# Offsets of both axes in one load, the fourth convolution behind the first batch, and all column spreads on VectorE

## The reference, cut to what matters

```python
off = conv2d(x, ow, ob).reshape(Bn, K, 2, Hh, Ww)          # K = 9 taps, y and x offsets
cy = iy[None, None, :, None] + dy[None, :, None, None] + off[:, :, 0]
cx = ix[None, None, None, :] + dx[None, :, None, None] + off[:, :, 1]
# bilinear samples of x at (cy, cx), zero outside the image
samp = gather(y0i, x0i, (1 - wy) * (1 - wx)) + gather(y0i, x0i + 1, (1 - wy) * wx) \
     + gather(y0i + 1, x0i, wy * (1 - wx)) + gather(y0i + 1, x0i + 1, wy * wx)
out = jnp.einsum('bckhw,ock->bohw', samp, w.reshape(w.shape[0], Cin, K))
```

## Time and profile before

| | us |
|---|---|
| median of 3 executions | 921.49 (920.93 to 923.78) |
| profiled execution, its own time | 921.92 |
| its span | 919.9 |
| TensorE busy | 649.7 (71%) |
| VectorE busy | 579.8 (63%) |
| ScalarE busy | 467.0 (51%) |
| GpSimd busy | 376.6 (41%) |

### The profile page before, as it was taken

How to read it: one execution, slowest core, us unless ns; L and a number is a source line. 1 busy time by engine, 2 the same in 40 slices (tenths; PEclk the granted TensorE clock), 3 DMA queues, 4 the chain that set the end, 5 groups by cost and what they waited for, 6 DMA issues and landing times.

```text
span 919.9 us, 30354 instructions
## 1 busy us (share of the span) xinstructions
PE 649.7 (71%) x13944; PEld 451.3 (49%) x13944; DVE 579.8 (63%) x755; ACT 467.0 (51%) x623; POOL 376.6 (41%) x383
## 2 busy tenths in 40 slices
PE   2409999999987484758887379757875767909483
PEld 1104555567853373546666246436654555706252
DVE  6894162221344995758988434896886777677365
ACT  3505433432423765757778131675776777632513
POOL 6000000000038347897886003859778888300000
PEclk9858999999999897888888779988887878958787
DMA  4000000000079637664664007966556665000002
GB/s 152 0 0 2 2 4 3 2 16 4 16 182 280 238 115 247 218 209 155 222 210 148 1 2 193 343 197 215 193 164 233 217 217 201 26 0 4 1 3 92
DMA packets 37994, 108.76 MB, mean 118 GB/s; under 512 B 16244, under 2 KB 20980, under 8 KB 29672
## 3 DMA queue, kind: packets, MB, share of 16 engines
q0 software_dynamic: 23616, 86.82, 28.2%
q1 hardware_dynamic: 14248, 19.97, 7.0%
HBM read 91.84 MB, written 19.65 MB: 121 GB/s over the span
## 4 chain that ended last, share of the span: by engine, by line
PE 37%; DVE 24%; POOL 12%; DMA 11%; issue 8%; ACT 7%; SPq 0%; DVEq 0%; ACTq 0%; POOLq 0%
PE psum L1222 12%; DMA arena<-offsets_by_batch 10%; PE psum L1269 7%; POOL arena L1500 6%; POOL arena L417 6%; PE psum L1198 5%; PE psum L1303 4%; PE psum L1415 3%; DVE arena L729 3%; DVE arena L730 3%; DVE arena L728 2%; PE psum L1281 2%; PE psum L1422 2%; ACT arena L1068 1%; PE psum L1235 1%
## 5 line engine op out<-in xcount | busy, mean ns | idle before, releaser
L1303 PE MATMUL psum<-arena 64*64 64x297 f32 (+4 forms) x4512 | 237.4, 369 | 122.6 <-ACT arena L1078 94.4
L1303 PEld LDWEIGHTS psum<-arena 64*64 64x64 f32 x4512 | 185.3, 149 | 174.6 <-issue 112.9
L417 POOL TENSOR_SCALAR arena<-arena 128x384 f32<-128x384 f32 (+2 forms) x68 | 180.7, 2681 | 47.3 <-PE psum L1303 47.2
L1500 POOL DMA_DIRECT2D arena<-offsets_by_batch x256 | 151.2, 633 | 42.4 <-DVE arena L730 33.1
L1471 POOL DMA_DIRECT2D columns<-arena x16 | 10.1, 757 | 298.3 <-DVE arena L694 243.3
L1222 PE MATMUL psum<-arena 32*32 32x512 f32 x3456 | 115.0, 597 | 0.3 <-DVE arena L652 0.3
L728 DVE SCALAR_TENSOR_TENSOR arena<-arena 128x792 f32<-128x792 f32 (+3 forms) x96 | 94.0, 979 | 25.3 <-ACT arena L1068 24.8
L1055 ACT ACTIVATE arena<-arena 128x2304 f32<-128x2304 f32 (+1 forms) x32 | 71.5, 2235 | 60.5 <-DMA arena<-offsets_by_batch 60.5
L1269 PE MATMUL psum<-arena 32*32 32x512 f32 x2304 | 86.3, 641 | 21.8 <-issue 16.0
L1067 ACT ACTIVATE arena<-arena 128x792 f32<-128x792 f32 (+3 forms) x96 | 84.5, 880 | 33.4 <-DMA arena<-offsets_by_batch 33.4
L1078 ACT ACTIVATE arena<-psum 128x792 f32<-128x792 f32 (+1 forms) x96 | 82.7, 861 | 32.4 <-PE psum L1303 25.2
(11 more groups left out here) (138 smaller groups left out, 688.9 us busy)
## 6 DMA issues: line engine op xcount, KB each, us to landing
arena<-offsets_by_batch POOLq DMA_DIRECT2D x224, 288.0 KB, 5.2
arena<-offsets_by_batch POOLq DMA_DIRECT2D x32, 312.0 KB, 5.7
offsets<-arena SPq DMA_DIRECT2D x32, 256.0 KB, 7.8
offsets_by_batch<-offsets SPq DMA_DIRECT2D x92, 48.0 KB, 2.8
columns<-arena POOLq DMA_DIRECT2D x8, 320.0 KB, 6.7
arena<-columns POOLq DMA_DIRECT2D x8, 320.0 KB, 7.5
arena<-in_x SPq DMA_DIRECT2D x4, 512.0 KB, 5.3
out<-arena SPq DMA_DIRECT2D x8, 256.0 KB, 2.2
```

The lines of the kernel that those rows point to most:

```text
L417: return eng.tensor_scalar(ap(z_at(a, 0) + i * C, [[64, NBK], [ZROW, b - a], [1, C]]), ap(ZC + c % 2 * ZCS + (a - CHUNKS[c][0]) * C, [[ZCB ...
L1303: ins = t_.matmul(ps_t(s, bank + r, first * K * w, many * K * w), window, ap(g_at(unit, d0) + first * TW + s * w, [[GS + TW, many], [SLOTS ...
L1500: g.dma_start(cols(in_at(n, axis), in_rows(n) * W, 64 * r + 32 * half, 32), bass.AP(batch_d.tensor, (axis * B + 4 * r) * NB * INS + n * IN ...
```

## The change

Three things are edited.

1. *One load for both axes.* In DRAM the arranged offsets of a batch now hold x and y side by side, and so does the buffer on chip (`in_at`). `load_batch` issues four transfers of 576 KB instead of eight of 288 KB, on one semaphore (`s_in`), and ScalarE's distances wait for all of it. `arrange_batch` issues one copy per axis: six for a batch in the middle instead of three.
2. *The fourth convolution.* TensorE runs `convolve(3)` between the units of batch 0 and those of batch 1. ScalarE copies it out behind unit 2 and the y terms of unit 6. VectorE takes its reach and bounds behind batch 1 instead of behind batch 0. It has bank 4 like the third one, and its bounded offsets go to a place of their own (`bounded_at`), so that they no longer wait for the store of quarter 1. SyncE arranges batch 4 ahead of the store of quarter 3. ScalarE waits for the store and the reach of quarter 3 at unit 24 instead of unit 6.
3. *The spreads.* All four images are spread by VectorE, `for i in range(4)`. GpSimd has no arithmetic left in the loop; it issues `load_batch(n)` and, behind the loads of batches 4 and 8, `load_windows`.

```diff
@@ -207,11 +207,16 @@
         NATS = 4 * CH
         assert 8 * CH <= SPAR and 2 * NATS <= min(N, SPAR)
 
+        def bounded_at(m):
+
+
+            return RAW + NATS if m == 3 else D1 + m % 2 * NATS
+
         PROJ = T_PAD[3] + PADN - 2 * CH
 
         xt_d = nc.dram_tensor("columns", [2, XQ, 4, H, C], F32, kind="Internal").ap()
         off_d = nc.dram_tensor("offsets", [2, B * KP, H, W], F32, kind="Internal").ap()
-        batch_d = nc.dram_tensor("offsets_by_batch", [2, B, NB, INS], F32, kind="Internal").ap()
+        batch_d = nc.dram_tensor("offsets_by_batch", [B, NB, 2 * INS], F32, kind="Internal").ap()
         flag_d = nc.dram_tensor("reach", [P, 8], F32, kind="Internal").ap()
 
         psum = ctx.enter_context(nc.psum_tensor("psum", [P, 8, CH], F32))
...
@@ -298,7 +302,7 @@
 
         def conv_bank(m):
 
-            return 4 if m % 2 == 0 else 0
+            return 0 if m == 1 else 4
 
         HALF = N // 2
         HALF_ROWS = H // 2 + 2
...
@@ -463,9 +467,11 @@
 
                 def taps(ky, at, step, row, rows):
 
-                    sp.dma_start(bass.AP(batch_d.tensor, n * INS + at, [[NB * INS, 2 * B], [step, 3], [1, rows * W]]),
-                                 bass.AP(off_d.tensor, 3 * (ky + 1) * N + row * W,
-                                         [[KP * N, 2 * B], [N, 3], [1, rows * W]])).then_inc(s_ar[n % 2], 16)
+                    for axis in range(2):
+                        sp.dma_start(bass.AP(batch_d.tensor, (2 * n * ER + axis * in_rows(n)) * W + at,
+                                             [[2 * NB * INS, B], [step, 3], [1, rows * W]]),
+                                     bass.AP(off_d.tensor, (axis * B * KP + 3 * (ky + 1)) * N + row * W,
+                                             [[KP * N, B], [N, 3], [1, rows * W]])).then_inc(s_ar[n % 2], 16)
 
                 for ky in (-1, 0, 1):
                     row = SLOTS * n - ky
...
@@ -493,8 +499,8 @@
                 arrange_batch(L, 2)
                 store_offsets(L, 2)
                 arrange_batch(L, 3)
+                arrange_batch(L, 4)
                 store_offsets(L, 3)
-                arrange_batch(L, 4)
                 sp.wait_ge(s_am, L + 1)
                 sp.dma_start(flag_d, cols(FMAX, 8)).then_inc(s_fd, 16)
                 for n in range(4, NB):
...
@@ -697,9 +703,11 @@
             def bound_offsets(L, m):
 
                 dve.wait_ge(s_cve, 16 * L + 4 * m + 4)
-                if m >= 2:
-                    dve.wait_ge(s_ds[m - 2], 64 * (L + 1))
-                raw, d1 = RAW + m % 2 * NATS, D1 + m % 2 * NATS
+                if m == 2:
+                    dve.wait_ge(s_ds[0], 64 * (L + 1))
+                if m == 3:
+                    dve.wait_ge(s_red, 4 * L + 4)
+                raw, d1 = RAW + m % 2 * NATS, bounded_at(m)
                 link(v.tensor_scalar(cols(d1, NATS), cols(raw, NATS), con("minus_limit"), con("limit"), ALU.max,
                                      ALU.min))
                 v.tensor_tensor(ap(d1, [[W, 4 * 8], [1, W]], 0, 64), ap(d1, [[W, 4 * 8], [1, W]], 0, 64),
...
@@ -707,6 +715,7 @@
 
             def reach(L, m):
 
+                dve.wait_ge(s_cve, 16 * L + 4 * m + 4)
                 ins = v.tensor_reduce(cols(FM + m * 32, 32), ap(RAW + m % 2 * NATS, [[W, 32], [1, W]]), AX.X, ALU.max,
                                       apply_absolute_value=True)
                 ins.then_inc(s_red, 1)
...
@@ -737,7 +746,7 @@
                 dve.wait_ge(s_zc[c % 2], 128 * L + 64 * (c // 2 + 1))
                 dve.wait_ge(s_un, UNITS * L + NU * max(n - 1, 0))
                 for a, b in parts:
-                    for i in (2, 3):
+                    for i in range(4):
                         ins = spread_part(v, c, a, b, i)
                 ins.then_inc(s_zv, 1)
 
...
@@ -899,9 +908,9 @@
                     if n < 2:
                         spread_windows(L, n)
                     batch(L, n)
-                    if n == 0:
+                    if n == 1:
+                        reach(L, 3)
                         bound_offsets(L, 3)
-                        reach(L, 3)
                     j = n // 2 - 2
                     if n % 2 == 0 and j >= 1:
                         add_shared_rows(L, j)
...
@@ -1050,7 +1059,7 @@
 
             def distances(L, n):
 
-                act.wait_ge(s_inx[n % 2], in_count(L, n))
+                act.wait_ge(s_in[n % 2], in_count(L, n))
                 tx = cols(in_at(n, 0), in_rows(n) * W)
                 a.activation(tx, tx, ACT.Abs, bias=con("minus_q")).then_inc(s_u, 1)
 
...
@@ -1101,20 +1109,23 @@
                     copy_columns(L, g_)
                 copy_offsets(L, 1)
                 copy_offsets(L, 2)
-                for unit in range(RING - 1):
+                for unit in range(RING):
                     y_terms(L, unit)
-                copy_offsets(L, 3)
-                y_terms(L, RING - 1)
                 act.wait_ge(s_xs[0], 64 * (L + 1))
                 act.wait_ge(s_xs[1], 64 * (L + 1))
                 for unit in range(UNITS):
                     if unit == 2 * NU:
-                        for m in range(4):
+                        for m in range(3):
                             act.wait_ge(s_ds[m], 64 * (L + 1))
+                        act.wait_ge(s_red, 4 * L + 3)
+                    if unit == 4 * 2 * NU:
+                        act.wait_ge(s_ds[3], 64 * (L + 1))
                         act.wait_ge(s_red, 4 * (L + 1))
                     copy_samples(L, unit)
                     if unit + RING < UNITS:
                         y_terms(L, unit + RING)
+                    if unit == NU - 1:
+                        copy_offsets(L, 3)
                     n, u = divmod(unit, NU)
                     if u == 1 and n % 2 == 0 and n >= 2:
                         copy_rows(L, n // 2 - 1)
...
@@ -1347,10 +1357,11 @@
                 pe.wait_ge(s_xtv, 4 * L + 4)
                 convolve(2)
                 pe.wait_ge(s_cve, 16 * L + 8)
-                convolve(3)
-                pe.wait_ge(s_cve, 16 * (L + 1))
                 pe.wait_ge(s_ws, 16)
                 for unit in range(UNITS):
+                    if unit == NU:
+                        pe.wait_ge(s_cve, 16 * L + 12)
+                        convolve(3)
                     sample(unit)
                     n, u = divmod(unit, NU)
                     if u == 0 and n % 2 == 0 and n >= 2:
...
@@ -1447,19 +1458,6 @@
             g.memset(cols(W_OUT, NGRP * Q), 0.0).then_inc(s_woz, 1)
 
 
-            def spread_windows(L, n):
-
-                c, parts = window_rows(n)
-                pool.wait_ge(s_zc[c % 2], 128 * L + 64 * (c // 2 + 1))
-                if n >= 2:
-                    pool.wait_ge(s_un, UNITS * L + NU * (n - 1))
-                elif L == 1:
-                    pool.wait_ge(s_un, UNITS * L)
-                for a, b in parts:
-                    for i in range(2):
-                        ins = spread_part(g, c, a, b, i)
-                ins.then_inc(s_zx, 1)
-
             def store_columns(L, part):
 
                 first, end = ((0, 20), (20, 32))[part]
...
@@ -1494,12 +1491,12 @@
                 pool.wait_ge(s_ar[n % 2], arranged(L, n))
                 if n >= 2:
                     pool.wait_ge(s_g, UNITS * L + NU * (n - 1))
-                for axis, done in ((0, s_inx[n % 2]), (1, s_iny[n % 2])):
-                    for half in range(2):
-                        for r in range(2):
-                            g.dma_start(cols(in_at(n, axis), in_rows(n) * W, 64 * r + 32 * half, 32),
-                                        bass.AP(batch_d.tensor, (axis * B + 4 * r) * NB * INS + n * INS,
-                                                [[0, QW // 2], [NB * INS, 4], [1, in_rows(n) * W]])).then_inc(done, 16)
+                for half in range(2):
+                    for r in range(2):
+                        g.dma_start(cols(in_at(n, 0), 2 * in_rows(n) * W, 64 * r + 32 * half, 32),
+                                    bass.AP(batch_d.tensor, 2 * (4 * r * NB + n) * INS,
+                                            [[0, QW // 2], [2 * NB * INS, 4], [1, 2 * in_rows(n) * W]])
+                                    ).then_inc(s_in[n % 2], 16)
 
             pool.wait_ge(s_zp, 64)
             for L in range(2):
...
@@ -1512,9 +1509,8 @@
                 for n in range(NB):
                     if n >= 2:
                         load_batch(L, n)
-                    spread_windows(L, n)
-                    if n in (3, 7):
-                        load_windows(L, (n + 1) // 4 + 1)
+                    if n in (4, 8):
+                        load_windows(L, n // 4 + 1)
 
             pool.wait_ge(s_xa, 3 * NCH)
             g.memset(ap(XP3, [[PW, 4 * RP], [PW - 1, 2]]), 0.0)
```

16 lines of the change are left out of this document (6 added, 10 removed).

## The result

The change made the kernel slower. The median is 934.49 us (932.18 to 937.31), against 921.21 us for the kernel before on the same chip. The ratio is 1.0149, with a 95% interval of 1.0103 to 1.0195. The profiled executions have spans of 930.4 and 919.9 us. The forecast was 912 us and the range ended at 924, so both were missed, and the sign too.

What follows compares the result with a forecast made beforehand. The prediction took a chain through GpSimd's spreads and the offset landing as the bound. Loops (-8.1, -9.0), layer starts (+1.7, +5.2) and last batches (+1.2) summed to -9.0 us: 912 us, range 899 to 924.

Steps and rivals of the forecast that it cites:

- What bounds the kernel: Sampling stage: a chain going round, no full engine; GpSimd's 7 us of spreads delay each load, then the landing follows.
- The loop: Steady-state loop of two batches: 24.35 us against 26.07, gaining 8.1 and 9.0 us in the two layers.
- issue and landing of the whole load ... I take 10.2: Loop term from first issue to last landing of the merged load: 10.2 us, bounded by 9.2 and 11.8.
- I cost them at nothing: Windows issued behind a load in the loop: no cost, as the next load leaves 6 us later.
- The distances behind the landing: Loop term on ScalarE: 2.2 us of distances now follow the whole landing, since x and y share one semaphore.
- VectorE with four spreads: Loop term on VectorE from first product to last, with two added spreads of 0.66 us: 9.25 us.
- The start of layer 0: First batches of the first layer: VectorE idles 6.6 us after batch 1; batch 2 ends 8.6 us behind, batch 4 1.7.
- The start of layer 1: First batches of the second layer: batch 2 ends 10.5 us behind, batch 4 5.2 us behind.
- The merged wait costs more than GpSimd's spreads did: Rival, chance 0.25: ScalarE's distances wait for both axes; landing at 10.9 or above, 921 us at 10.85, 928 at 11.3.
- The rival of a shorter landing: Offset loads, chance 0.20: half the issues queue bytes up to 2.2 us sooner; 898 us at a 9.2 us landing.
- SyncE's extra copies: Layer starts, rival, chance 0.02: copies delay every load by more than 3 us of room, loops gain nothing, 930 us.
- The signs to look for: Profile after: GpSimd without arithmetic, load waits at distances, pairs of 24 to 25 us, VectorE idle some 6 us behind batch 1.

Runs made afterwards that it cites:

- e1_spreads_only: Kernel before with only the spreads moved, all four images on VectorE; loads and convolutions as before: 875.90 us, ratio 0.9513.
- e7_half_bytes: Changed kernel, but from the third load on only the x half of the offsets is loaded, y terms using old ones: 874.24 us.
- e4_eight_issues: Changed kernel with its layout and single semaphore, but each offset load cut into eight transfers of 288 KB, x first: 922.76 us.
- e6_wait_both: e1_spreads_only with one more wait, so that the distances of x also wait for y; transfers unchanged: 905.23 us.
- e9_conv_only: Kernel before with only the later fourth convolution, its copies, reach and bounds behind batches 0 and 1: 930.88 us, ratio 1.0107.
- e3_no_conv: Changed kernel with the fourth convolution back in front of the samples, its reach and bounds behind batch 0: 914.98 us.
- e5_double_copies: e1_spreads_only with SyncE's copies split by axis, six a batch instead of three, layout and loads untouched: 877.22 us.
- e10_merge_only: Kernel before with only the merged load, x and y in one load and one wait: 969.62 us, ratio 1.0517.

## Why the prediction was wrong

**What bounds the kernel: right, its size in a pair too large.** GpSimd's spreads stand ahead of the load in its queue, and the landing behind them. e1_spreads_only shows that 45 us were to be had from the first and e7_half_bytes that the second sets what is left. But the prediction says that the buffer "was free long before" and that 7 us are on the path in every pair. In the timeline of VectorE of the kernel before, the product that frees the buffer is

```profile
445.59 0.90 DVE L730 SCALAR_TENSOR_TENSOR arena<-arena 128x720 f32<-128x720 f32 x1
```

It ends at 446.49, so without the spreads the load of 449.72 would leave at about 447.2, 2.5 us sooner and not 7. The pairs of e1_spreads_only are 3.0 us shorter (23.0 against 26.07). The sum of the loop did not use the 7 us and is not hurt by it.

**The loop: wrong, and the step that failed is "issue and landing of the whole load ... I take 10.2".** The ten loads inside the two loops took 10.8, 14.2, 12.3, 12.2 and 12.4 us in layer 0 and 12.0, 13.8, 11.0, 12.2 and 12.4 us in layer 1, from the first issue to the distances, a mean of 12.3. That is above the upper end of the bound, 11.8. The release (0.7 for 0.9) and the products (9.15 for 9.25) came out 0.3 us lower together. So a loop is 2.1 - 0.3 = 1.8 us longer than forecast, 18 us in ten loops; the table has 18.9. Three things are in the 2.1 us:
- *Four large transfers land later than eight small ones.* The prediction argued that fewer issues could only help. e4_eight_issues shows the reverse: 12 us over 14 loads, 0.9 us each. For transfers of twice the size there was no row; the bound was made from loads in pieces of 288 KB.
- *Windows behind a load.* The two loads of 14.2 and 13.8 us are those that have windows issued behind them. The timeline of GpSimd:

```profile
394.51 2.89 POOL L1496 DMA_DIRECT2D arena<-offsets_by_batch  x4 [11.94 <-DVE arena L739]
400.46 2.56 POOL L1483 DMA_DIRECT2D arena<-columns  x4 [3.06 <-DVE arena L421]
```

  and of ScalarE:

```profile
408.75 2.21 ACT L1064 ACTIVATE arena<-arena 128x2304 f32<-128x2304 f32 x1 [6.95 <-DMA arena<-offsets_by_batch]
```

  "I cost them at nothing", because the next load leaves 6 us later. But it is the load in front, still landing, that they share the DMA engines with. The pair with windows took 27.94 us, the other four of its layer (131.39 - 27.94) / 4 = 25.86: 2.1 us a layer. In e4_eight_issues too the longest load is the one with windows behind it (13.7 us, issued at 393.96). This part was only read from traces; no run moved the windows alone.
- *The rest*, about 0.7 us. Half of it is there without the merge: in e1_spreads_only the seven loads of the loops without windows in which the y terms wait for the landing took 9.8 to 11.3 us to the first y term, 10.55 in the mean, where the prediction took 10.2, half a microsecond under 10.7. The other half is what e4_eight_issues has above that (10.9); no run says where it comes from.

**The distances behind the landing: right in size, wrong in weight.** The prediction had the 2.2 us in its sum and called the merge "about 2 us a pair". e6_wait_both measured 29 us for the wait alone. What the sum did not show is how the two halves of the change compare. By the same terms, the loop without the merge is 0.9 + 10.7 + 1.8 + 9.25 = 22.65 us, against e1's 22.7 and 23.3. So the prediction's own terms give (26.07 - 22.65) x 10 = 34 us for the spreads in ten loops, and (24.35 - 22.65) x 10 = 17 us that the merge gives back. The merge was a pure loss by these terms already; measured, it cost 39 us beside the spreads. The prediction summed only the two together, and a small difference of two large numbers is no safer than the worse of them.

**VectorE with four spreads: right.** 9.15 us from the first product to the last, 9.25 forecast. L421 takes 1.41 us for four.

**The start of layer 0: the sum near, by luck, as two terms were wrong against each other.** Timelines of GpSimd, ScalarE and VectorE of the changed kernel:

```profile
305.48 3.70 POOL L1496 DMA_DIRECT2D arena<-offsets_by_batch  x4 [17.74 <-DVE arena L739]
```

```profile
318.72 2.21 ACT L1064 ACTIVATE arena<-arena 128x2304 f32<-128x2304 f32 x1 [7.61 <-DMA arena<-offsets_by_batch]
...
322.50 2.41 ACT L1057 ACTIVATE arena<-psum,arena 128x512 f32<-128x512 f32 x4
```

```profile
324.94 2.29 DVE L719 TENSOR_REDUCE arena<-arena 128x32 f32<-128x2048 f32 x1 [9.51 <-ACT arena L1057]
...
331.15 1.35 DVE L731 TENSOR_SCALAR arena<-arena 128x2304 f32<-128x2304 f32 x1
...
341.69 1.35 DVE L731 TENSOR_SCALAR arena<-arena 128x2304 f32<-128x2304 f32 x1
```

Load 2 left at 305.48, not at 310.4: batch 0 began sooner, its x term at 294.51 against 298.31 before, and the prediction put that gain at next to nothing. The convolution's going is one reason (295.54 in e9_conv_only) and not the only one: with the convolution where it was, the x term starts at 295.73 in e3_no_conv and at 294.02 in e5_double_copies. The load then took 13.2 us instead of 10.2. The copies follow at 322.5 and VectorE waits 9.5 us for them; the prediction had this wait, with 6.6 us. Batch 2 ends at 341.69, 6.1 us behind the earlier trace rows, forecast 8.6. Batch 4 ends 2.5 us behind, forecast 1.7.

**The start of layer 1: right.** From batch 15 of layer 0 to batch 5 of layer 1 the change costs 5.7 us, forecast 5.2 and 0.6 for the last batch. e9_conv_only shows what share is edit 2's: the first stretch of the table is 3.5 us longer than before, that from batch 15 to batch 5 is 7.9 us, and the two loops (128.54 and 127.75 us) give 4.4 back. So edit 2 was a loss by itself, 7.0 us between these profiled executions and 10 between the medians, and not only a cost of the start that the loops would pay for; the prediction never put its price apart.

**The rivals.** "The merged wait costs more than GpSimd's spreads did" came true, with the mechanism and the place that were given, and beyond its worst case of 11.8. It had a chance of 0.25. The rival of a shorter landing was wrong in its direction. The Trainium skill, DMA: Bandwidth & Descriptors, Anatomy of one DMA, had stood beside it: its fit gives an estimate of 7.4 us for a load, and the loops of the changed kernel show 10.8 to 14.2. SyncE's extra copies cost nothing that can be told (e5_double_copies). The spreads did not hold up the issues, as they come 4 us after the load is released; but issues beside another VectorE instruction, the x term, are longer, as the last section shows.

**The signs to look for.** GpSimd without arithmetic, all of ScalarE's load waits at the distances, and VectorE's idle time behind batch 1 were there. Batch 2 ended 6.1 us later after the start of layer 0 and 11.0 after that of layer 1 (15.0 less the 4.0 that were lost before it), where 8 to 11 were forecast. A pair of 24 to 25 us, and the same with windows and without, were not.

## What to carry to other kernels

Price each part of a change as if it were made alone, with the same terms, before adding them: here the best kernel is one of the three parts by itself, 875.9 us against 921 before and 934 with all. Fewer and larger transfers were not complete sooner here, where what waits is the last byte; and where an instruction can start on the first half of a load, one semaphore for both halves puts that instruction behind the whole landing, in each round. A cost taken at "nothing" must be checked against the transfer already in flight, not only against the next one. And work on one engine that runs beside another's costs only the part that goes on after the other is done: 7 us of spreads on GpSimd were worth 3 us a pair.

## What the runs showed of the hardware

- *Shape of a transfer.* With the same bytes, destination and source rows, loads in pieces of 32 partitions and 288 KB ran at about 400 GB/s and landed 5.0 us after issue (median), pieces of 64 partitions and 576 KB at about 230 GB/s and 9.9 us. The Trainium skill, DMA: Bandwidth & Descriptors, Rules for kernel authors, advises 128 partitions and at least 1 MiB per DMA for the most bandwidth; no offset load here was tried in that size or over 128 partitions. For this source, which is read again for each group of four partitions, the step from 32 to 64 partitions and from 288 to 576 KB lowered the rate. The 576 KB pieces of the changed kernel, over 32 partitions, took 7.6 us.
- *Issues beside VectorE.* Four issues take 2.76 us when they start together with VectorE's x term (448.72, beside its batch start at 448.44), and 2.13 us when VectorE is idle (459.65). The Trainium skill, SBUF — State Buffer, SBUF: two separate sides, says that a two-port VectorE instruction keeps GpSimd from writing the descriptors of its DMAs; the 0.6 us agrees with it, though no row shows whether the x term is such an instruction. The kernel before agrees too: its seven issues of 1.6 to 1.8 us, where the median is 0.58, all begin within 0.4 us of the start of an x term. In the loops of both layers, the issues that start with an x term took 2.37 to 2.89 us, and they are the ones that the round waits for. No run had the x term elsewhere.
- *GpSimd beside VectorE.* The same two spreads took GpSimd 4.09 us at 454.12 in the kernel before and 6.97 us in the earlier trace rows, 8.31 us at 388.71 of the same trace, and 8.31 us at 427.74 of e10_merge_only, while VectorE's four take 1.41 us.
